# Attention stage on one Trainium2 core: moving VectorE's output statistics and first-tile work between its copies of turned probabilities

## What is computed

```python
x = _layernorm(x + _L0_attn_ref(x, ...))                       # Mamba-2 mixer, then a gated MLP
x = _layernorm(x + _L0_xattn_ref(x, ctx_1024, ctx_1024, ...))  # cross attention, 16 heads of 32
x = _layernorm(x + _L0_ffn_ref(x, ...))                        # MLP with fp8-rounded activations
# _L0_xattn_ref:
q = (Q @ Wq.T + bq).reshape(b, vc, h, hd); k, v likewise from the context
atten = softmax(einsum('bqhd,bkhd->bhqk', q, k) / sqrt(hd), axis=3)
out = einsum('bhqd,bdhv->bqhv', atten, v).reshape(b, vc, d_model) @ Wo.T + bo
```

## Time and profile before

| | |
|---|---|
| time, median of 3 runs | 2718.32 us |
| time, the three runs | 2716.38, 2718.32, 3430.97 us |
| time of the profiled execution | 2718.93 us |
| its span (first to last instruction) | 2717.1 us |
| instructions | 42369 |
| attention stage in the span, about | 1587 to 2257 us |

### The profile page before, as it was taken

The page is one execution under the profiler, slowest core; times in us unless marked ns, Lnnn a source line. Parts: engine busy times, 40 slices in busy tenths (PEclk is TensorE's granted clock), DMA queues, the critical chain, the costliest instruction groups (busy, mean ns, idle before and its releaser), DMA issues.

```text
span 2717.1 us, 42369 instructions
## 1 busy us (share of the span) xinstructions
PE 2662.6 (98%) x15264; PEld 2070.6 (76%) x15264; DVE 1521.5 (56%) x2561; ACT 1019.4 (38%) x2375; POOL 692.7 (25%) x594
## 2 busy tenths in 40 slices
PE   7999999999999999999999989999999999999999
PEld 5777777777778888888888867777777767777776
DVE  8787797797795322331233277777777773111122
ACT  6344334334344222122212155555555553222221
POOL 5553553553552101000100101322233322000000
PEclk9999999999999999999999999999999999999999
DMA  4001001101114101110111221110111124211111
GB/s 154 21 27 47 28 18 46 37 9 46 44 48 143 62 1 62 62 62 0 62 62 34 82 67 55 63 45 24 62 54 62 58 67 150 79 46 46 46 46 47
DMA packets 85482, 147.83 MB, mean 54 GB/s; under 512 B 4032, under 2 KB 17984, under 8 KB 85408
## 3 DMA queue, kind: packets, MB, share of 16 engines
q1 hardware_dynamic: 85408, 146.84, 15.7%
HBM read 113.27 MB, written 33.55 MB: 54 GB/s over the span
## 4 chain that ended last, share of the span: by engine, by line
PE 89%; DVE 7%; issue 2%; ACT 1%; DMA 0%; DVEq 0%; SPq 0%; POOL 0%; ACTq 0%; POOLq 0%
PE ps L75 23%; PE ps L77 23%; PE ps L76 23%; PE ps L1813 4%; PE ps L2176 4%; PE ps L816 2%; PE ps L1825 2%; PE ps L1804 2%; DVE mx_m L608 1%; DVE mx_cv L600 1%; PE ps L792 1%; PE ps L804 1%; PE ps L747 1%; PE ps L844 1%; PE ps L1756 1%
## 5 line engine op out<-in xcount | busy, mean ns | idle before, releaser
L1507 ACT ACTIVATE at_pr<-ps,at_nm 128x256 f32<-128x256 f32 x512 | 235.5, 472 | 203.8 <-DVE at_nm L1661 203.8
L1183 DVE TENSOR_TENSOR gm_m_lo<-gm_m,gm_m_hi 128x512 fp32r<-128x512 f32 (+1 forms) x88 | 60.9, 692 | 416.9 <-ACT gm_m_hi L1100 416.9
L75 PE MATMUL ps<-sh_u_hi,gm_gu_hi 128*128 128x512 f32 (+1 forms) x704 | 274.7, 390 | 0.0
L76 PE MATMUL ps<-sh_u_lo,gm_gu_hi 128*128 128x512 f32 (+1 forms) x704 | 274.6, 390 | 0.0
L77 PE MATMUL ps<-sh_u_hi,gm_gu_lo 128*128 128x512 f32 (+1 forms) x704 | 274.6, 390 | 0.0
L1667 DVE COPY at_pT<-ps 128x512 f32<-128x512 f32 x256 | 176.0, 687 | 139.7 <-PE ps L1813 137.8
L1094 ACT ACTIVATE gm_sg<-ps 128x512 f32<-128x512 f32 (+1 forms) x88 | 52.7, 598 | 517.8 <-PE ps L77 517.6
L543 POOL TENSOR_TENSOR mx_m<-mx_m,mx_g 128x512 f32<-128x512 f32 x128 | 185.4, 1449 | 86.6 <-DVE mx_m L610 86.4
L75 PE MATMUL ps<-sh_u_hi,qm_w_hi 128*128 128x512 f32 x512 | 201.4, 393 | 2.1 <-issue 1.1
L77 PE MATMUL ps<-sh_u_hi,qm_w_lo 128*128 128x512 f32 x512 | 199.4, 389 | 0.0
L76 PE MATMUL ps<-sh_u_lo,qm_w_hi 128*128 128x512 f32 x512 | 199.2, 389 | 0.0
(11 more groups left out here) (253 smaller groups left out, 6350.7 us busy)
## 6 DMA issues: line engine op xcount, KB each, us to landing
sh_xf<-x_scratch SPq DMA_DIRECT2D x16, 1024.0 KB, 7.4
mx_xr<-in_x SPq DMA_DIRECT2D x8, 1024.0 KB, 6.2
h_scratch<-mx_xr SPq DMA_DIRECT2D x8, 1024.0 KB, 5.0
sh_xf<-h_scratch SPq DMA_DIRECT2D x8, 1024.0 KB, 8.1
gm_xr<-in_x SPq DMA_DIRECT2D x8, 1024.0 KB, 7.3
gm_r<-h_scratch SPq DMA_DIRECT2D x8, 1024.0 KB, 6.2
x_scratch<-gm_r SPq DMA_DIRECT2D x8, 1024.0 KB, 5.1
at_cf<-in_ctxT SPq DMA_DIRECT2D x16, 512.0 KB, 3.7
```

The costliest lines, as they stand in the source:

```text
L75: nc.tensor.matmul(out, l_hi, r_hi, start=first, stop=False)
L76: nc.tensor.matmul(out, l_hi, r_lo, start=False, stop=False)
L1507: A(pr[h][:, t, :], SC[h][:, SEQ * t:SEQ * t + SEQ], ACT.Exp, bias=nm[:, 4 * n + h, t:t + 1], accum_out=sums[:, 2 * b + t, 4 * g + h:4 * g ...
```

## The change

Only DVE's program in the attention stage changes. No instruction is added or removed; three kinds of work move to other places in the same groups or in later ones:

- step 0, groups 0 to 3: the low part of a wo piece goes from the group's end to between the copies of heads 0 and 1, the normalisation of a gm block to between the copies of heads 1 and 2
- steps 1 to 7: the four bn_stats go from the ends of groups 3, 4 (two) and 5 to between the copies of heads 0 and 1 of groups 3, 4, 5 and 6
- steps 1 to 7: the four bn_aggr go from the end of group 5 to between the copies of heads 0 and 1 of group 7

```diff
                 take_pT(i, n, 0)
+                if step_0(i):
+                    if n < TT:
+                        wt.low(dve, 13 + n)
+                elif 3 <= n < 7:
+                    statistics(i - 1, n - 3, before(i, n + 2) + 1)
+                elif n == 7:
+                    gather(i - 1)
                 take_pT(i, n, 1)
+                if step_0(i) and n < TT:
+                    prev.norm(dve, NP - 1, n)
                 if n == 0 and not step_0(i):
                     normalise(i - 1, HG - 1)
...
                 if has(i, 2 * n + 1, more):
                     take(i, 2 * n + 1)
-                if step_0(i) and n < TT:
-                    wt.low(dve, 13 + n)
-                    prev.norm(dve, NP - 1, n)
-                if not step_0(i):
-                    if n == 3:
-                        statistics(i - 1, 0, before(i, 5) + 1)
-                    elif n == 4:
-                        for t in range(1, 3):
-                            statistics(i - 1, t, before(i, 5 + t) + 1)
-                    elif n == 5:
-                        statistics(i - 1, 3, before(i, 8) + 1)
-                        gather(i - 1)
```

## The result

The changed kernel takes 2787.03 us (median of 6 runs, 2785.79 to 2791.14), the kernel before 2718.47 us beside it (6 runs; one of them, at 3430.97 us, was a slow execution, and the ratio leaves it out). The ratio is 1.0254 with a 95% interval of 1.0241 to 1.0267: slower by 68.6 us, where 69.4 were predicted. The profiled execution took 2786.09 us with a span of 2784.3 us, 67.2 us longer than the 2717.1 of before. Behind the edit of DVE's program, the same lines of code stand three lines higher: the turns of the next tile are L1753, the turns of probabilities L1810, `values` L1822, the spread L1835.

A forecast was written before the change was run, and what follows sets the result against it. PE bounds the kernel, busy 98% of the span. Stalls 51.0, handover 12.0, clock 11.9 and step 0 at 0, less gains 5.5, make 69.4 us on 2718.9: 2788 us, range 2768 to 2806.

The forecast's parts named there:

- The six stalls: Group 1, steps 2 to 7: PE waits 8.5 us for late xf ahead of its first turn, 51.0 us in all.
- 6.2 us of slack against a shift of 14.7: xf landed 6.2 us before PE's first turn in group 1 needed it; the bn_aggr moves 14.7 us later.
- The handover: End of step 7: late store and weight loads delay ACT, and PE's spread stalls 12.0 us, bounds 9 to 16.
- The clock: Behind the seven new stalls PE's clock falls, costing 1.7 us each, 11.9 us in all, bounds 0 to 24.
- Rival 1: Stalls come, but the clock keeps full rate and the handover costs about 6 us: 2770 us, chance 0.15.
- Rival 3: Step 0's waits for ACT do not balance and the clock costs twice as much: 2804 us, chance 0.11.
- The gains: PE's gaps close: 3.4 us over steps 1 to 6 and 2.1 in step 7, together 5.5 us, bounds 3 to 7.
- Step 0: Groups 0 to 3: DVE's waits for ACT's high part balance the freed row maxima, 0 us, bounds -1 to +4.
- Rival 2: xf is in time, no turn waits and only the gains remain: 2713 us, chance 0.04.

The follow-up runs named there:

- The filler: Changed kernel with 37 throwaway matmuls on PE ahead of the first turn in group 1 of steps 1 to 7: 2782.64 us, ratio 1.0241.

## Why the prediction was right, point by point

**The six stalls, 51.0 predicted: 50.6 measured.** The step that decided was to follow DVE, POOL and SP in their orders and set 6.2 us of slack against a shift of 14.7. The move of the bn_aggr alone gave 50.5, its return none.

**The handover, 12.0 predicted: 11.2 measured.** ACT's timeline of the changed kernel:

```profile
2312.95 1.28 ACT L214 ACTIVATE qm_w_hi<-qm_stage 128x512 fp32r<-128x512 f32 x2 [17.56 <-DMA qm_stage<-in_w1T]
2314.14 0.57 ACT L1513 ACTIVATE at_rT<-ps 32x512 fp32r<-32x512 f32 x1
```

The copy that the spread needs stands behind the rounding of two weight pieces, which stands behind SP's late store and `r`, as the prediction had it. POOL's last low part, which I gave nothing, cost nothing.

**The clock, 11.9 predicted: 15.3 measured.** From the first turn in group 1 to the second the kernel before takes 6.66 us in every step; the changed one takes 9.13, 9.39, 9.48, 7.96, 8.80 and 9.10, which is 13.9 us more, 2.3 a gap and not 1.7. Behind the spread it is 1.4 more (7.11 us against 5.67 to the next output-projection matmuls). The filler's 12.9 against that 13.9 is a second measure of the same term. The mechanism held and the size was too small by 3.4 us: I took the price of a partly idle stretch of step 0 for gaps without any work. The Trainium skill, "TensorE: Matmul & The Clock Gate", part 1 with its thin-M example, has PE pay after every wait in a loop; by that rule all seven stalls pay, and the trace agrees: each of the seven was followed by matmuls 0.43 us apart, at a price of 1.3 to 2.8 us. Rival 1, a clock that keeps its rate and a handover of 6 us, is refuted by the 0.57 behind the gap, by the throwaway matmuls and by the 11.2 us of the spread's wait. Rival 3 asked for 24 us of clock and 4 us more in step 0; the clock cost 15.3 and step 0 nothing.

**The gains, 5.5 predicted: 7.9 measured.** Steps 1 to 6 gained 1.0 us each, 6.05 in all: from the second turn of one step to the first of the next it was 75.13 us and is 82.5 less the stall, 74.1. I had counted PE's two visible gaps, 0.57 us. Laid beside each other, the two PE timelines of step 3 put the gain at three places: 0.23 us at `values` in group 5, 0.47 at `values` in group 6, and 0.29 at the turn of head 1 in group 6, which stood behind the copy of head 0. That third place hardly shows as idle time of PE, since the matmul ahead was still running; its weight load had waited 0.56 us in the kernel before:

```profile
1900.53 0.42 PEld L1813 LDWEIGHTS ps<-sh_ident,at_pr 128*128 128x128 f32 x4 [0.56 <-DVE at_pT L1667]
```

Step 7 gained 1.84 where 2.1 were predicted.

**Step 0, 0 predicted: 1.1 us shorter in the changed kernel's trace, no difference in the times of step 0 alone.** DVE does wait for ACT's high part ahead of the low part:

```profile
1593.16 0.69 DVE L225 TENSOR_TENSOR at_wo_lo<-at_o,at_wo_hi 128x512 fp32r<-128x512 f32 x1 [1.78 <-ACT at_wo_hi L214]
...
1623.54 0.69 DVE L225 TENSOR_TENSOR at_wo_lo<-at_o,at_wo_hi 128x512 fp32r<-128x512 f32 x1 [1.57 <-ACT at_wo_hi L214]
```

The waits and the freed end of each group balance: step 0 alone took 2718.05 us where the kernel before took 2719.19 beside it, a difference inside its interval. The 1.1 us of the trace is no more than two executions of the same step 0 differ by: in the kernel with the bn_aggr alone it was 1.6 us shorter than in the kernel before, because the clock stayed at 1.00. The version with the two pieces swapped was 3.4 us faster (2709.43 to 2706.07); how much of that is the waits and how much the clock is open.

**The sum.** 50.6 + 11.2 + 15.3 - 7.9 - 1.1 = 68.1 us, and 0.9 less in the stages ahead of attention: 67.2, the difference of the spans. The prediction's 69.4 was near it partly by luck: 3.4 us too little for the clock and 3.5 too little for the gains (2.4 of them in the steps, 1.1 in step 0) cancelled. Two terms of the sum were thus mis-sized: a slow stretch behind a gap, put at 1.7 us, measured 2.3, and the gain of a step, put at 0.57 us, measured 1.0.

**Rival 2** was that `xf` is in time when SP issues it ahead of the store. The run with that order had none of those waits, so the mechanism was named rightly, and it needed an edit of SP's program that the change does not make. Its other condition, a shift below the slack of 6.2 us, was met by the bn_aggr in the middle of group 6 (5.4 us by the expectation), and there too no turn waited.

## What to carry to other kernels

Before an instruction is moved to a place where its own engine is idle, follow what its result releases, through every queue in order, to the first transfer or product that has a due time, and set the shift against the slack there: 0.37 us of DVE work, moved by 14.7 us, cost 77 us. Price an idle gap of PE of 2 us or more as the gap plus a stretch at the lower clock, here 1.3 to 2.8 us. And when something is issued earlier, look at what else it starts early, and what that then meets.

## What the runs showed of the hardware that I had not expected

**Small DVE instructions stand still beside POOL.** A CAST of 128x16 elements takes 0.17 us alone and 1.18 beside POOL's additions, the subtraction that follows 0.18 alone and 1.21 beside POOL's low part; each ended within 0.03 us of the POOL instruction that it met. The 128x512 copies of PSUM beside the same additions kept their 0.69 us. The Trainium skill, "SBUF — State Buffer", section "Who interferes with whom", says that DVE and GpSimd have one port pair in common, locked for a whole instruction, for DVE's copies and casts in their two-port modes and for DVE instructions with two SBUF inputs against GpSimd instructions that read SBUF. The trace agrees in the two that stood still, which read SBUF alone, and in the copies, which read PSUM; that the CAST ran in a two-port mode no run shows. It does not agree everywhere. Beside POOL's normalisation, in the kernel that loads ahead of the store, the CAST waited for the end of one block (2.07 us each, from 1750.43 on), but the subtraction behind it took 0.20 us while POOL's next block was already running:

```profile
1750.43 6.20 POOL L1605 TENSOR_SCALAR at_r<-at_r,at_mv,at_rstd 128x512 f32<-128x512 f32 x3 [0.18 <-POOL at_rstd L948]
...
1752.08 0.46 DVE L1691 CAST at_r_hl<-at_rinv 128x16 fp32r<-128x16 f32 x1
1752.57 0.20 DVE L1693 TENSOR_TENSOR at_r_hl<-at_rinv,at_r_hl 128x16 fp32r<-128x16 f32 x1
```

Why it was let through the runs do not show. Where the DVE instruction does stand still, the meeting costs what is left of POOL's instruction, up to 1.2 us here, for 16 elements a partition. The kernel before had such meetings already: in group 5 of steps 1 to 6 its CAST took 0.82 to 0.84 us and ended 0.03 us behind POOL's low part. In the changed kernel it comes later against POOL and takes 0.35 us there.

**A short gap costs nearly as much clock as a long one.** Ahead of the turns, gaps of 3.1 to 3.5 us were followed by losses of 1.3 to 1.6 us, gaps of 8.3 to 8.5 us by 1.3 to 2.8. Ahead of the spread, a gap of 2.3 us (the bn_aggr in the middle of group 6) lost 1.7 us, one of 5.7 us 1.7, and gaps of 11.2 to 11.4 us in five kernels 1.4 to 2.3. The idle gaps of 0.12 to 0.41 us in the kernel before's steps 1 to 6 left the granted clock at 1.00.
